# A message-passing layer on one core: TensorE's signals in the main loop carried by a drain instead of by the last matmul

## The chip, the cores and the metric

The kernel runs on one core of a Trainium2 chip. The metric is the device time of the whole program in microseconds (us), lower is better. A time is compared as the median of several runs.

The engines are called as the profile calls them: PE is TensorE (its matmuls; PEld its weight loads), DVE is VectorE, ACT is ScalarE, POOL is GpSimd, SP is SyncE, which here only issues transfers. Engines run side by side and are held together by semaphores: an instruction may wait until a semaphore has reached a value, and may raise one when it is done.

## The reference

One graph layer on 12,500 nodes of 64 features and 400,000 edges, sorted by their target node, all in f32:

```python
m_in = jnp.concatenate([x[src], x[dst], edge_attr], axis=-1)
h = jax.nn.silu(m_in @ W1 + b1)
messages = jax.nn.silu(h @ W2 + b2)
agg = jax.ops.segment_sum(messages, dst, num_segments=x.shape[0])
node_in = jnp.concatenate([x, agg], axis=-1)
u = jax.nn.silu(node_in @ W3 + b3)
y = x + u
out = (y - mean(y)) / sqrt(var(y) + 1e-5)
```

## The kernel before

The edges are taken in groups of 1024 (8 tiles of 128 edges): 390 full groups and a shorter last one, 391 in all. Everything of a group lies in a window of 48 target nodes, so the target's part of the first layer comes from a small table (`w_in`, reloaded for each group by SP) and a one-hot of 48 columns. Of a group's eight tiles of source rows `x[src]`, most are fetched by POOL with one indirect DMA per tile (seven for most groups, L547); the eighth is computed on PE: a one-hot of the source's row (`rows_T`) times the whole node table (`parts`), and DVE then picks the wanted slice out of the product (`kept`). In every twelfth group one more tile is fetched row by row by transfers that ACT issues (L674). An edge buffer `edge_in` has 12 slots, so POOL may be up to 12 groups ahead; before it refills a slot it waits for `s_in_T`, the signal of the transposes that read the slot last (`refill`, L567).

PE's step for group g is written out by hand and stands in this order:

```python
first_layer(0, g + 1)
transpose_inputs(0, g + 2)
pieces(g)
wait_for_pair(0, g)
second_layer(0, g + 1)
spread_keys(...)      # in 350 of the steps
update(...)           # a few steps per 24
sum_messages(0, g)
```

Each part ends in a signal. With the names of the rows further down (`z_ps` stands for both `z1_ps` and `z2_ps`):

- `transpose_inputs` (L1099, `in_ps`): 8 transposes; `s_in_T` lets ACT copy them out (`in_T`, L638) and POOL refill the slot.
- `first_layer` (L1120 and L1121): 2 matmuls of 512 columns into the two halves of the partitions; `s_z1` lets ACT apply the first silu (L642).
- `second_layer` (L1126): 4 matmuls; `s_z2` lets DVE add the bias (L855), ACT apply the second silu (L646), and DVE sum the messages in three passes (L866, L871, L875, L878, which makes `pair`).
- `spread_keys` (L1138): 1 matmul; `s_keys` lets DVE make the one-hot `rows_T` (L908).
- `sum_messages` (L1148): 2 small matmuls; `s_agg` lets DVE add them to `sums` (L886).
- `pick_piece` (L1165): each of the 350 computed tiles takes 26 matmuls in 13 pieces and two rounds; `s_round` at the end of a round lets DVE read it (L920, L924, which makes `kept`). A round goes to one of three PSUM banks, and its first piece waits for `s_picked`, DVE's reading of the round three before.

An f32 matmul stands in the trace as two instructions, the one-pass matmuls of `pick_piece` as one. Every engine issues in order. DVE's step for group g: bias of g + 1, `sums` of g, one-hots of g + 4, the three passes of g + 1, then `rows_T`, and the reading of the rounds.

Of the kernel before, what the change touches and what calls it, by code (L numbers as in the profile page):

```python
# [23 lines left out]
def gnn_layer(nc, x, src, dst, edge_attr, W1, b1, W2, b2, W3, b3, out):  # L24
# [3 lines left out]
    P = 128  # L28
    N, H = x.shape
# [12 lines left out]
    OH, XS, EA = slice(0, WIN), slice(WIN, WIN + H), slice(WIN + H, P)  # L42
# [11 lines left out]
    S = 12  # L54
    CH = 8
    RING = 3
    NW = 6
# [24 lines left out]
    PARTS = 2  # L82
    ROW_SETS = 3
    HB = C // H
    ROUNDS = 2
    PICK_BANKS = 3
# [43 lines left out]
    def picked(g):  # L130
        return g in PICK_OF
# [6 lines left out]
    def fetched(g):  # L138
        return g % S == 0 and 2 * S <= g < FULL
# [10 lines left out]
    def rows_landed(k, v):  # L150

        def upto(g):
            return sum(tiles_of(h) for h in range(g % S, g + 1, S))
        return 16 * upto(k * B + v)

    ctx = ExitStack()
    with ctx:
        def sb(name, shape, dt=F32):
            return ctx.enter_context(nc.sbuf_tensor(name, shape, dt))

        def pb(name, banks=()):
            return ctx.enter_context(nc.psum_tensor(name, [P, *banks, C], F32))

        def sem(name):
            return ctx.enter_context(nc.semaphore(name))
# [5 lines left out]
        parts = sb("parts", [P, PARTS, NT, H], F32R)  # L171
        edge_in = sb("edge_in", [P, S, T, P])
# [19 lines left out]
        w_in = sb("w_in", [P, NW, H])  # L192
# [30 lines left out]
        ident_r = sb("ident_r", [P, P], F32R)  # L223
        hot_place = [sb("hot_place0", [P, 2, CH, HB]), sb("hot_place1", [P, 2, CH, HB], I32)]
        kept = sb("kept", [P, HB, H])
        rows_T = sb("rows_T", [P, ROW_SETS, SETS, P], F32R)

        dst_rel = sb("dst_rel", [P, 2, CH, T])
        in_T = sb("in_T", [P, 2, C])
# [4 lines left out]
        pair = sb("pair", [P, 2, 2, H])  # L234
# [12 lines left out]
        z1_ps = pb("z1_ps")  # L247
        z2_ps = pb("z2_ps")
        agg_ps = pb("agg_ps")
        pick_ps = [pb(f"pick_ps{i}") for i in range(PICK_BANKS)]  # L250
# [34 lines left out]
        s_in_T = sem("edge_in_transposed")  # L285
        s_in_c = sem("edge_in_copied")
        s_z1 = sem("z1_done")
        s_h = sem("h_done")
        s_z2 = sem("z2_done")
# [7 lines left out]
        s_agg = sem("window_summed")  # L297
# [6 lines left out]
        s_keys = sem("keys_spread")  # L304
        s_rowsT = sem("rows_T_made")
        s_round = sem("round_done")
# [64 lines left out]
        def done(k, v):  # L371

            return k * B + (v + 1)
# [5 lines left out]
        def fetch_of(g):  # L379

            n = g // S - 2
            return n % 2, n // 2
# [681 lines left out]
        def _(pe):  # L1064
# [4 lines left out]
                             start=True, stop=True).then_inc(s_base, 1)  # L1069
# [5 lines left out]
            for n in range(len(BANKS) + 1):  # L1075
                if n < len(BANKS):
                    a, b = BANKS[n]
                    if n >= 2:
                        pe.wait_ge(s_xTc, n - 1)
                    for j in range((b - a) // 2):  # L1080
                        last = nc.tensor.transpose(in_ps[:, n % 2, j * P:(j + 1) * P],
                                                   xs[:, a + 2 * j:a + 2 * j + 2, :].rearrange("p k f -> p (k f)"), ident[:, :])
                    last.then_inc(s_xT, 1)
                if n:
                    a, b = BANKS[n - 1]
# [3 lines left out]
                    for j in range((b - a) // 2):  # L1089
                        last = nc.tensor.matmul(pick_ps[(n - 1) % 2][:, j * 2 * P:(j + 1) * 2 * P],  # L1090
                                                in_T[:, (n - 1) % 2, j * P:(j + 1) * P],
                                                w_node[:, :, :, :].rearrange("p a b f -> p (a b f)"), start=True, stop=True)
# [4 lines left out]
            def transpose_tiles(s):  # L1097
                for t in range(T):
                    last = nc.tensor.transpose(in_ps[:, t // HT, t % HT * P:(t % HT + 1) * P],  # L1099
                                               edge_in[:, s, t, :], ident[:, :])  # L1100
                return last

            def transpose_inputs(k, v):


                pe.wait_ge(s_oh, done(k, v))
                pe.wait_ge(s_eac, done(k, v))
                pe.wait_ge(s_xg[v % S], rows_landed(k, v))
                if picked(k * B + v):
                    pe.wait_ge(s_row, PICK_OF[k * B + v] + 1)  # L1110
                if fetched(v):
                    j, before = fetch_of(v)
                    for odd in range(2):
                        pe.wait_ge(s_fetched[j][odd], (before + 1) * (P // 2 * 16))
                transpose_tiles(v % S).then_inc(s_in_T, 1)

            def first_layer(k, v):
                pe.wait_ge(s_win[v % NW], k * (16 * (B // NW)) + 16 * (v // NW + 1))
                pe.wait_ge(s_in_c, done(k, v))
                nc.tensor.matmul(z1_ps[0:H, :], w_in[:, v % NW, :], in_T[:, 0, :], start=True, stop=True)  # L1120
                nc.tensor.matmul(z1_ps[H:P, :], w_in[:, v % NW, :], in_T[:, 1, :], start=True, stop=True).then_inc(s_z1, 1)  # L1121

            def by_edges():

                for c in range(HT):
                    last = nc.tensor.matmul(z2_ps[:, c * P:(c + 1) * P], h_T[:, c * P:(c + 1) * P], w2_bd[:, :],  # L1126
                                            start=True, stop=True)
                return last

            def second_layer(k, v):  # L1130
                pe.wait_ge(s_h, done(k, v))
                by_edges().then_inc(s_z2, 1)

            def spread_keys(n):

                c = TARGET[n] // CH
                pe.wait_ge(s_found, (c - TARGET[0] // CH) * 2 + 2)
                nc.tensor.matmul(agg_ps[:, KEYS], find_key[:, c % 2, TARGET[n] % CH:TARGET[n] % CH + 1].to_broadcast([P, P]),  # L1138
                                 ident_r[:, :], start=True, stop=True).then_inc(s_keys, 1)

            def wait_for_pair(k, v):

# [2 lines left out]
            def sum_messages(k, v, tail=False):  # L1145

                for i, tile in ((0, 0), (1, TT - 1 if tail else T - 1)):
                    last = nc.tensor.matmul(agg_ps[i * H:(i + 1) * H, OH], pair[:, v % 2, i, :], edge_in[:, v % S, tile, OH],  # L1148
                                            start=True, stop=True)
                last.then_inc(s_agg, 1)  # L1150

            def pick_piece(n, piece):

                r, c = PIECES[piece]
                at = n * ROUNDS + r
                a = c * PLACES + r * HB
                b = min(NT, a + HB)
                if piece == 0:
                    pe.wait_ge(s_rowsT, n + 1)
                if c == 0 and at >= PICK_BANKS:  # L1160

                    pe.wait_ge(s_picked, at - PICK_BANKS + 1)
                done_with = (r, c + 1) not in PIECES
                for j in range(PARTS):
                    last = nc.tensor.matmul(pick_ps[at % PICK_BANKS][:, 0:(b - a) * H], rows_T[:, n % ROW_SETS, c, :],  # L1165
                                            parts[:, j, a:b, :].rearrange("p k f -> p (k f)"),
                                            start=(c == 0 and j == 0), stop=(done_with and j == PARTS - 1))
                if done_with:
                    last.then_inc(s_round, 1)

            def pieces(g):
                for piece in range(PICKS * NP):
# [100 lines left out]
```

## Time and profile before

| | |
|---|---|
| time, median of 3 runs | 4534.21 us (4520.94 to 4543.54) |
| span of the profiled execution, first to last instruction | 4497.7 us |
| PE busy | 3654.5 us, 81% |
| DVE busy | 2757.0 us, 61% |
| POOL busy | 2591.6 us, 58% |
| ACT busy | 1046.2 us, 23% |

The profile gives of its execution only the span, not a device time of its own. The median of the runs is 36.5 us above the span; that is taken as what lies around it. Busy time is work that the trace records. Ends of matmuls are modelled, and where a matmul's record ends later than the next one starts, the two are pipelined.

### The profile page before, as it was taken

To read this page: it belongs to the slowest core of one execution; us is meant where nothing else is said; L and a number is where in the kernel's file an instruction comes from. 1 tells how busy PE (TensorE), PEld (TensorE's weight loads), DVE (VectorE), ACT (ScalarE), POOL (GpSimd) and SP (SyncE) were. 2 spreads that over 40 slices of the span, in tenths; PEclk is the share of its full clock that TensorE was granted. 3 is DMA by queue.
4 is the path that set the end of the run, shared out by engine and by line. 5 is a ranking of instruction groups with operands and counts; after the bars stand their busy time and mean duration, and the time that the engine had idled before them with its cause. 6 is when DMAs were issued, how large, how long until landed. Compare 5 with 4: busy or idle time off the path is not lost. (4 is left out here: it accounts for less than half of the span.)

```text
span 4497.7 us, 68074 instructions
## 1 busy us (share of the span) xinstructions
PE 3654.5 (81%) x19180; PEld 2747.4 (61%) x19180; DVE 2757.0 (61%) x4834; ACT 1046.2 (23%) x1714; POOL 2591.6 (58%) x2754
## 2 busy tenths in 40 slices
PE   1588888888888888888888888888888888888888
PEld 1366666666666666666666666666666666666665
DVE  2366666666666666666666666665665666666667
ACT  0222222222222222222222222222222222222223
POOL 7365655556555655656555555555555555555650
PEclk6789999999999999999999999999999999999998
DMA  4211111111111111111111111111111111111110
GB/s 100 59 29 34 32 28 34 33 34 29 34 33 28 34 34 30 32 28 39 28 34 28 35 32 28 33 33 33 28 33 34 28 33 28 34 32 28 38 23 11
DMA packets 335197, 150.34 MB, mean 33 GB/s; under 512 B 224958, under 2 KB 290527, under 8 KB 334822
## 3 DMA queue, kind: packets, MB, share of 16 engines
q0 software_dynamic: 87808, 90.09, 9.5%
q1 hardware_dynamic: 237238, 54.50, 5.7%
q8 instruction: 159, 2.61, 0.2%
q10 hardware_dynamic: 9776, 1.37, 0.2%
q14 instruction: 216, 1.77, 0.1%
HBM read 136.10 MB, written 9.62 MB: 32 GB/s over the span
## 5 line engine op out<-in xcount | busy, mean ns | idle before, releaser
L547 POOL DMA_INDIRECT edge_in<-in_x_dram,src_i x2744 | 2590.4, 944 | 1789.7 <-issue 743.5
L1165 PE MATMUL pick_ps<-parts,rows_T 128*128 128x512 f32 (+1 forms) x9100 | 2298.7, 405 | 564.0 <-issue 268.6
L1165 PEld LDWEIGHTS pick_ps<-parts,rows_T 128*128 128x128 f32 x9100 | 1698.8, 196 | 993.7 <-issue 384.4
L646 ACT ACTIVATE z_ps<-z_ps,zero_col 128x512 f32<-128x512 f32 x391 | 258.9, 662 | 2859.1 <-DVE z_ps L855 1975.8
L855 DVE TENSOR_TENSOR z_ps<-z_ps,b_rep 128x512 f32<-128x512 f32 x391 | 272.4, 697 | 920.9 <-remote 553.3
L1099 PEld LDWEIGHTS in_ps<-ident,edge_in 128*128 128x128 f32 x3128 | 347.7, 144 | 362.1 <-issue 341.6
L1126 PEld LDWEIGHTS z_ps<-w_bd,h_T 128*128 128x128 f32 x3128 | 471.4, 219 | 145.6 <-DVE pair L878 82.8
L1126 PE MATMUL z_ps<-w_bd,h_T 128*128 128x128 f32 x3128 | 485.7, 306 | 81.0 <-DVE pair L878 61.1
L1120 PE MATMUL z_ps<-in_T,w_in 128*64 128x512 f32 x782 | 441.2, 646 | 19.8 <-issue 14.1
L1099 PE MATMUL in_ps<-ident,edge_in 128*128 128x128 f32 x3128 | 442.4, 286 | 13.9 <-issue 7.7
L1121 PE MATMUL z_ps<-in_T,w_in 128*64 128x512 f32 x782 | 442.4, 649 | 8.6 <-issue 8.5
L638 ACT COPY in_T<-in_ps 128x1024 f32<-128x1024 f32 x391 | 394.5, 1009 | 70.9 <-remote 56.9
L908 DVE TENSOR_TENSOR rows_T<-agg_ps,key_of 128x896 fp32r<-128x896 f32 x350 | 378.6, 1082 | 0.0
L926 DVE TENSOR_REDUCE edge_in<-kept 128x64 f32<-128x512 f32 x350 | 367.8, 1051 | 12.1
L866 DVE TENSOR_REDUCE every<-z_ps 128x64 f32<-128x512 f32 x391 | 267.7, 685 | 142.0 <-ACT z_ps L646 107.6
L886 DVE TENSOR_TENSOR sums<-sums,agg_ps 128x48 f32 x391 | 79.7, 204 | 447.7 <-remote 418.2
L642 ACT ACTIVATE h_T<-z_ps,b_col 128x512 f32<-128x512 f32 x391 | 267.7, 685 | 359.3 <-remote 320.3
L871 DVE TENSOR_TENSOR z_ps<-z_ps,beyond 128x512 f32<-128x512 f32 x391 | 273.5, 699 | 13.4
L875 DVE TENSOR_REDUCE pair<-z_ps 128x64 f32<-128x512 f32 x391 | 270.2, 691 | 13.4
L924 DVE COPY_PREDICATED kept<-hot_place,pick_ps 128x512 f32<-128x512 int32 x350 | 253.6, 725 | 19.2 <-remote 4.2
L920 DVE TENSOR_TENSOR kept<-pick_ps,hot_place 128x512 f32<-128x512 f32 x350 | 239.8, 685 | 23.9 <-remote 7.3
L841 DVE TENSOR_TENSOR edge_in<-agg_ps,dst_rel 128x384 f32<-128x384 f32 x391 | 214.6, 550 | 0.4 <-issue 0.4
(104 smaller groups left out, 1231.5 us busy)
## 6 DMA issues: line engine op xcount, KB each, us to landing
edge_in<-in_x_dram ACTq DMA_DIRECT2D x3968, 0.2 KB
edge_in<-in_x_dram,src_i POOLq DMA_INDIRECT x2744
ea<-in_edge_attr_dram SPq DMA_DIRECT2D x48, 512.0 KB
w_in<-node_terms SPq DMA_DIRECT2D x391, 12.0 KB
node_terms<-h_T SPq DMA_DIRECT2D x12, 256.0 KB
node_terms<-lot_T SPq DMA_DIRECT2D x12, 256.0 KB
y<-in_x_dram SPq DMA_DIRECT2D x15, 192.0 KB
term<-node_terms SPq DMA_DIRECT2D x15, 192.0 KB
```

Source lines behind the costliest of these rows:

```text
L547: pool.indirect_dma_start(out=edge_in[:, to_slot, t, XS], out_offset=None, in_=x[:, :], in_offset=bass.IndirectOffsetOnAxis(ap=indices[:, ...
L638: nc.scalar.copy(in_T[:, :, :], in_ps[:, :, :]).then_inc(s_in_c, 1)
L855: nc.vector.tensor_add(z2, z2, b2_rep[:, :].unsqueeze(1).to_broadcast([P, T, H])).then_inc(s_biased, 1)
L871: nc.vector.tensor_mul(messages, messages, beyond[:, v // CH % 2, v % CH, :].rearrange("p (a c) -> p c a", a=2).unsqueeze(3).to_broadcast( ...
L875: nc.vector.tensor_reduce(pair[:, v % 2, 1, :], z2_ps[:, :].rearrange("p (k f) -> p f k", f=H), AX.X, ALU.add).then_inc(s_other, 1)
L908: nc.vector.tensor_tensor(rows_T[:, n % ROW_SETS, :, :], agg_ps[:, KEYS].unsqueeze(1).to_broadcast([P, SETS, P]), key_of[:, :].unsqueeze(2 ...
L926: nc.vector.tensor_reduce(edge_in[:, TARGET[n] % S, PICKED, XS], kept[:, :, :].rearrange("p k f -> p f k"), AX.X, ALU.add).then_inc(s_row, 1)
L1099: last = nc.tensor.transpose(in_ps[:, t // HT, t % HT * P:(t % HT + 1) * P], edge_in[:, s, t, :], ident[:, :])
L1120: nc.tensor.matmul(z1_ps[0:H, :], w_in[:, v % NW, :], in_T[:, 0, :], start=True, stop=True)
L1121: nc.tensor.matmul(z1_ps[H:P, :], w_in[:, v % NW, :], in_T[:, 1, :], start=True, stop=True).then_inc(s_z1, 1)
L1126: last = nc.tensor.matmul(z2_ps[:, c * P:(c + 1) * P], h_T[:, c * P:(c + 1) * P], w2_bd[:, :], start=True, stop=True)
L1165: last = nc.tensor.matmul(pick_ps[at % PICK_BANKS][:, 0:(b - a) * H], rows_T[:, n % ROW_SETS, c, :], parts[:, j, a:b, :].rearrange("p k f ...
```

## The change

Inside the main loop the semaphore increments of `transpose_inputs`, `first_layer`, `second_layer`, `spread_keys`, `sum_messages` and the ends of the rounds in `pick_piece` no longer stand on the last matmul. A drain of PE is issued behind the matmuls and carries the increment. A drain is an instruction of PE's own sequencer: it is done when the engine has finished everything before it, and what stands behind it is issued after it. The matmuls, their order, their waits and all other engines stay as they are; so do the update matmuls (`update`), and everything before the loop. Lines behind the first drain move down by one to four in the changed file.

```diff
-                transpose_tiles(v % S).then_inc(s_in_T, 1)
+                transpose_tiles(v % S)
+                pe.drain().then_inc(s_in_T, 1)
...
-                nc.tensor.matmul(z1_ps[H:P, :], w_in[:, v % NW, :], in_T[:, 1, :], start=True, stop=True).then_inc(s_z1, 1)
+                nc.tensor.matmul(z1_ps[H:P, :], w_in[:, v % NW, :], in_T[:, 1, :], start=True, stop=True)
+                pe.drain().then_inc(s_z1, 1)
...
-                by_edges().then_inc(s_z2, 1)
+                by_edges()
+                pe.drain().then_inc(s_z2, 1)
...
                 nc.tensor.matmul(agg_ps[:, KEYS], find_key[:, c % 2, TARGET[n] % CH:TARGET[n] % CH + 1].to_broadcast([P, P]),
-                                 ident_r[:, :], start=True, stop=True).then_inc(s_keys, 1)
+                                 ident_r[:, :], start=True, stop=True)
+                pe.drain().then_inc(s_keys, 1)
...
-                last.then_inc(s_agg, 1)
+                pe.drain().then_inc(s_agg, 1)
...
                 if done_with:
-                    last.then_inc(s_round, 1)
+                    pe.drain().then_inc(s_round, 1)
```

## Rows read from the trace of the kernel before

**Rows 1.** The page: the span, and each engine's busy time.

```profile
span 4497.7 us, 68074 instructions
PE 3654.5 (81%) x19180; PEld 2747.4 (61%) x19180; DVE 2757.0 (61%) x4834; ACT 1046.2 (23%) x1714; POOL 2591.6 (58%) x2754
```

**Rows 2.** Timeline, where the loop begins: start us, us, instruction [idle before <-releaser].

```profile
166.75 1.97 PE L1099 MATMUL in_ps<-ident,edge_in 128*128 128x128 f32 x8 [6.18 <-DVE edge_in L841]
```

**Rows 3.** Stretches: length, busy us (instructions) of PE, PEld, DVE, ACT, POOL; clock.

```profile
2300.00:3300.00 1000.00, 842.16 (x4413) 631.44 (x4413) 625.34 (x1091) 230.03 (x376) 589.81 (x625) 0.93 0.15 32
...
4386.50:4437.50 51.00, 50.57 (x290) 38.84 (x289) 40.02 (x66) 17.08 (x27) 0.00 (x0) 1.00 0.01 3
```

**Rows 4.** Waits of PE, 300 to 4376 us: total us, times, longest.

```profile
PE pick_ps L1165 <- DVE kept L920: 147.8, 50, 8.6
```

**Rows 5.** Timeline, one step inside the gathers.

```profile
321.56 1.05 PE L1126 MATMUL z_ps<-w_bd,h_T 128*128 128x128 f32 x8
...
322.54 0.32 PE L1148 MATMUL agg_ps<-edge_in,pair 128*64 128x48 f32 x4
...
323.66 1.09 PE L1099 MATMUL in_ps<-ident,edge_in 128*128 128x128 f32 x8
...
324.92 0.70 DVE L855 TENSOR_TENSOR z_ps<-z_ps,b_rep 128x512 f32<-128x512 f32 x1 [3.09 <-remote]
324.97 0.95 POOL L547 DMA_INDIRECT edge_in<-in_x_dram,src_i  x1 [0.30 <-issue]
...
327.83 0.69 ACT L642 ACTIVATE h_T<-z_ps,b_col 128x512 f32<-128x512 f32 x1 [1.51 <-remote]
327.87 0.20 DVE L886 TENSOR_TENSOR sums<-sums,agg_ps 128x48 f32 x1 [2.25 <-remote]
...
328.65 0.94 POOL L547 DMA_INDIRECT edge_in<-in_x_dram,src_i  x1 [2.73 <-remote]
...
332.03 1.17 PE L1165 MATMUL pick_ps<-parts,rows_T 128*128 128x512 f32 x4 [2.88 <-DVE kept L924]
```

**Rows 6.** Timeline, one step after the last gather.

```profile
4385.69 1.09 PE L1099 MATMUL in_ps<-ident,edge_in 128*128 128x128 f32 x8
...
4391.97 1.05 PE L1126 MATMUL z_ps<-w_bd,h_T 128*128 128x128 f32 x8
...
4392.78 0.30 PE L1138 MATMUL agg_ps<-ident_r,find_key 128*128 128x128 f32 x1
...
4393.01 0.32 PE L1148 MATMUL agg_ps<-edge_in,pair 128*64 128x48 f32 x4
4393.06 0.70 DVE L855 TENSOR_TENSOR z_ps<-z_ps,b_rep 128x512 f32<-128x512 f32 x1 [1.31 <-PE z_ps L1126]
...
4393.16 0.61 PE L1120 MATMUL z_ps<-in_T,w_in 128*64 128x512 f32 x1
...
4393.62 0.59 PE L1121 MATMUL z_ps<-in_T,w_in 128*64 128x512 f32 x1
...
4394.14 1.09 PE L1099 MATMUL in_ps<-ident,edge_in 128*128 128x128 f32 x8
...
4394.99 5.59 PE L1165 MATMUL pick_ps<-parts,rows_T 128*128 128x512 f32 x24
```

**Rows 7.** One line's instructions: duration ns min/median/max, first and last start.

```profile
L547 POOL DMA_INDIRECT edge_in<-in_x_dram,src_i x2744: 938/944/1323, 4.0 to 4381.2; - x196
L1165 PE MATMUL pick_ps<-parts,rows_T x9100: 218/396/797, 212.9 to 4450.3; 128*128 128x512 f32 x183, 128*128 128x128 f32 x15
```

**Rows 8.** Timeline: two places where PE restarts behind another engine's signal.

```profile
182.95 1.01 ACT L638 COPY in_T<-in_ps 128x1024 f32<-128x1024 f32 x1 [5.36 <-remote]
...
184.11 1.09 PE L1120 MATMUL z_ps<-in_T,w_in 128*64 128x512 f32 x1 [3.27 <-ACT in_T L638]
...
4484.16 0.06 DVE L1014 MEMSET done_mark<- 1x1 f32 x1
...
4484.27 3.68 PE L1181 MATMUL pick_ps<-w3a,sums 128*128 128x64 f32 x16 [0.52 <-DVE done_mark L1014]
```

More of the change, by code:

```diff
@@ L1147, in sum_messages @@
                 for i, tile in ((0, 0), (1, TT - 1 if tail else T - 1)):
-                    last = nc.tensor.matmul(agg_ps[i * H:(i + 1) * H, OH], pair[:, v % 2, i, :], edge_in[:, v % S, tile, OH],
-                                            start=True, stop=True)
-                last.then_inc(s_agg, 1)
+                    nc.tensor.matmul(agg_ps[i * H:(i + 1) * H, OH], pair[:, v % 2, i, :], edge_in[:, v % S, tile, OH],
+                                     start=True, stop=True)
+                pe.drain().then_inc(s_agg, 1)
             def pick_piece(n, piece):
@@ L1164, in pick_piece @@
                 for j in range(PARTS):
-                    last = nc.tensor.matmul(pick_ps[at % PICK_BANKS][:, 0:(b - a) * H], rows_T[:, n % ROW_SETS, c, :],
-                                            parts[:, j, a:b, :].rearrange("p k f -> p (k f)"),
-                                            start=(c == 0 and j == 0), stop=(done_with and j == PARTS - 1))
+                    nc.tensor.matmul(pick_ps[at % PICK_BANKS][:, 0:(b - a) * H], rows_T[:, n % ROW_SETS, c, :],
+                                     parts[:, j, a:b, :].rearrange("p k f -> p (k f)"),
+                                     start=(c == 0 and j == 0), stop=(done_with and j == PARTS - 1))
                 if done_with:
-                    last.then_inc(s_round, 1)
+                    pe.drain().then_inc(s_round, 1)
             def pieces(g):
```

## The prediction

> **What bounds the kernel now.** The page gives TensorE 3654.5 us of 4497.7, 81%, and no other engine over 61% [rows 1]. So PE is the busy engine, and yet it sits idle for 843 us. The loop begins at 166.8 us [rows 2] and ends where the last update matmuls begin, at 4484.3 [rows 8], so a group takes 4317.5 / 391 = 11.04 us on average.
>
> The view of stretches shows that it need not. From 4386.5 to 4437.5 us, after POOL's last gather [rows 3, 7], PE is busy 50.57 us of 51 at clock 1.00 and gets through 290 instructions, 5.7 in a us. In an ordinary stretch it is busy 842 of 1000 us at clock 0.93 and gets through 4413, or 4.4 in a us [rows 3]. The code of a step is the same in both. What differs is POOL: 590 us busy in 1000 there, 0 here.
>
> The timeline shows how POOL comes in. In the step without gathers, `second_layer` starts at 4391.97, ends by the record at 4393.02, and DVE's bias starts at 4393.06, 0.04 us later [rows 6]. In the step at 322 us `second_layer` ends at 322.61 and the bias starts at 324.92, after 3.09 us of idleness; `sum_messages` ends at 322.86 and DVE adds it at 327.87; the transposes end at 324.75 and POOL's next gather starts at 328.65, after 2.73 us of idleness [rows 5]. The last gather of that run of seven ended at 325.92, and ACT, DVE and POOL all move within 2 to 3 us of that. None of these waiters is waiting for anything but a PE signal, and PE was long past the matmul that carries it. The releaser "remote" says that no matching instruction lay near. So **while POOL issues gathers, signals carried by matmuls reach the others late by 2 to 5 us**, and in a bunch after the run.
>
> The circle closes through two waits. POOL starts the next run only on `s_in_T`, which is late until the run before is over. And DVE's reading of the rounds comes after the late bias in its own order, so PE's first piece of a round waits for `s_picked`: 2.88 us at 332.03 [rows 5], one of the waits that the list puts down to `kept` [rows 4]. Such an idle stretch also costs clock, 0.93 against 1.00 [rows 3]. A step without lateness takes 4394.14 - 4385.69 = 8.45 us with 24 pick instructions [rows 6]; the mean is 9100 / 391 = 23.3 [rows 7], each 5.59 / 24 = 0.23 us apart, so 8.29, and with the update matmuls (15 lots of 6, 180 instructions at up to 3.68 / 16 = 0.23 us [rows 8]; I take 25 us in all) 8.35 us. The lateness and what follows from it is worth 11.04 - 8.35 = 2.69 us a group, 1052 us in all.
>
> **What the change does, part by part.** It removes nothing from the matmuls. It adds per group four drains (transposes, first layer, second layer, sums), 350 / 391 for the keys and 700 / 391 for the rounds: 6.7 a group, 2614 in all.
>
> *What a drain costs on PE.* No drain stands in these rows, so it is built up. (a) The overlap is lost: the next matmul now starts before the record of the last one ends. From [rows 6]: second layer to keys 4393.02 - 4392.78 = 0.24; keys to sums 0.07 (times 0.9); sums to first layer 0.17; first layer to transposes 0.07; transposes to picks 0.24; within picks 0.396 [rows 7] less 0.23 = 0.17, times 1.8. Sum 1.09 us a group. (b) Restart: between a releasing instruction's end and PE's first matmul lie 0.05 us (4484.22 to 4484.27, the wait stands on the weight load) and 0.15 us (183.96 to 184.11, a separate wait before it) [rows 8]. A drain pays its own end and that restart, and the separate waits behind it, which PE's sequencer now works off while the matmuls in its queue still run, come into the open. Bounds: 0.1 us a drain (a restart alone) and 0.35 us (two restarts with a wait each, and 0.05). I take 0.2, since most drains have one separate wait behind them: 6.7 x 0.2 = 1.34 us. Together 2.43 us a group, 0.36 a drain; between 1.76 and 3.43.
>
> A rule speaks against the change here. The Trainium skill, "PSUM — Partial Sum Buffer", Engine vs sequencer instructions, says to put the increment on the matmul and to use a drain only for a standalone barrier, since it waits for the engine to go fully idle; the second half is what (a) and (b) charge for. It does not speak of late increments, and the trace does [rows 5].
>
> The drains lie wholly on PE's path, because PE is the engine that everyone waits for once signals are prompt; nothing hides them.
>
> *What the drains give.* The late signal is the one that a matmul carries. DVE's and ACT's own signals are taken up at once in the same stretch, and PE itself answers waits within 0.15 us, so I take it that an increment by PE's sequencer gets through during gathers. Then the 2.69 us go. What is late next: POOL has 7.02 gathers a group (2744 / 391) at 0.94 + 0.30 us [rows 5, 7], with about 0.7 us to start a run, 9.4 us, still under PE. DVE has 2757 / 391 = 7.1 us [rows 1]. So PE sets the pace, with no long idle stretch, at clock near 1.00.
>
> *The sum.* 8.35 + 2.43 = 10.78 us a group against 11.04: 391 x 0.26 = 102 us less. I give back 30 us for waits that stay (the first groups, ACT's row transfers in every twelfth). 4497.7 - 102 + 30 = 4426 of span, and with the 36.5 us around it **4460 us**, 1.6% under the median. By the bounds, 10.11 and 11.78 us a group, it is 4200 and 4850 us: two large terms of opposite sign nearly cancel.
>
> **The rivals.**
>
> *The restart is dear (slower).* Signals become prompt, but a drain and its restart cost over 0.28 us beside the overlap. The point from which it decides: 8.35 + 1.09 + 6.7 x = 11.04 gives x = 0.24 us. At 0.35 us it is 11.78 us a group, which is 290 us more than now and 30 on top: 4850. For it: in most steps one to three separate waits follow a drain. Against it: PE restarts in 0.05 to 0.15 us [rows 8].
>
> *The drain's increment is as late as the matmul's.* PE would not stand, but the circle stays and drains come on top, partly in idle time that PE has anyway (843 us less some 150 ahead of the loop, 1.8 us a group). About 12 us a group, or 375 us more: 4910. For it: I don't know which path is held. Against: PE's own matmuls run on at full rate while signals are held [rows 5], so what is held is the report, and the drain's report is another unit's.
>
> *The drain itself stands until the run of gathers is over.* Then the first drain in a run stops PE: a run of 7 x 1.25 us, 2 to 3 us behind it, and some 8 us of PE's work before the next run is released, 19 us a group: about 7700. It needs completion itself to be held, and PE's going on speaks against it.
>
> *The restart is cheap.* 0.1 us a drain or less, POOL's 9.4 us as the next bound: 4100 to 4220.
>
> **Chances.** Time differences under 0.5% (23 us) can't be told from none here. Forecast case 0.50 (of it 0.42 faster, 0.06 same, 0.02 slower; own range 4300 to 4590). Cheap restart 0.06. Dear restart 0.24 (0.02 of it same). Late drain 0.13 (0.01 same). Standing drain 0.07. That gives faster 0.48, same 0.09, slower 0.43. For the range I leave out the standing drain above and part of the cheap restart below: 4220 to 4950, which spans the bounds of the drain's cost.
>
> **What the profile after would show.** If the mechanism is right: POOL's, DVE's and ACT's waits with releaser "remote" are gone or small; the bias follows `second_layer` within 0.2 us in every stretch; PE's waits for `kept` are gone; the clock is near 1.00; between the parts of a step PE shows gaps of 0.1 to 0.5 us, at the drains; the stretch after the last gather gets slower, from 8.45 us a step to about 10.9, and equals the others. The last is the cleanest reading of a drain's price, (step - 8.45) / 7. If the stretch with gathers stays slower than the one without, signals are still held. The prediction is wrong by size if a drain costs other than 0.36 us; it is wrong by mechanism if the waiters' "remote" stays, or if PE stands for us at its drains.

## The result, and the profile after

The changed kernel takes 6359.06 us (median of 3 runs, 6339.75 to 6382.48) against 4534.21 us, a ratio of 1.404 [1.400, 1.408]: 1825 us slower, 40%. The forecast was 4460 us and the range ended at 4950.

The page of the kernel after: span and busy times, clock by fortieths of the span, and the head of the chain of work that ended last.

```profile
span 6380.6 us, 70688 instructions
PE 4669.6 (73%) x19180; PEld 3178.3 (50%) x19180; DVE 2760.7 (43%) x4834; ACT 1094.9 (17%) x1714; POOL 2594.4 (41%) x2754
...
PEclk7788788778887877887778877877888888877778
...
PEld 44%; issue 43%; PEldq 9%; DVE 2%; another core or an unknown queue 1%; DMA 0%; ACT 0%; ACTq 0%; PE 0%; DVEq 0%
```

The instructions of the engines are those of [rows 1], and 70688 - 68074 = 2614 more: the drains. PE does the same 19180 matmuls in 4669.6 us of busy time in place of 3654.5. One cause is the granted clock, 0.8 over the loop, where an ordinary stretch before had 0.93 [rows 3]; the other is that behind a drain the records no longer overlap. And 27% of the span it is idle. The chain runs almost wholly over PE (weight loads, its drains as PEldq, and "issue", time in which nothing that the profile shows is waited for).

The waits, whole span: total us, times, longest. PEq and PEldq are PE's sequencer; L1116 is the drain behind the transposes, L1135 the one behind `second_layer`, L1141 the matmul of `spread_keys`, which is the first one behind L1135.

```profile
POOL edge_in L547 <- PEq L1116: 2890.0, 373, 49.4
DVE z_ps L855 <- PEq L1135: 2777.6, 386, 19.3
...
PE agg_ps L1141 <- issue: 831.4, 349, 5.4
```

Inside the loop (300 to 6240 us) no "remote" is left: every waiter for PE now waits for a drain. But the waits are longer than before, and PE itself stands 831 us ahead of the keys' matmul, 2.4 us a time, behind the drain of `second_layer`.

One step of the timeline after, 3009 to 3030 us, with the matmuls of the picks left out:

```profile
3009.20 0.94 POOL L547 DMA_INDIRECT edge_in<-in_x_dram,src_i  x1 [0.30 <-issue]
...
3010.33 1.13 PE L1128 MATMUL z_ps<-w_bd,h_T 128*128 128x128 f32 x8 [2.06 <-issue]
...
3010.44 0.94 POOL L547 DMA_INDIRECT edge_in<-in_x_dram,src_i  x1 [0.30 <-issue]
...
3013.02 0.70 DVE L855 TENSOR_TENSOR z_ps<-z_ps,b_rep 128x512 f32<-128x512 f32 x1 [5.90 <-PEq L1135]
...
3013.19 0.45 PE L1141 MATMUL agg_ps<-ident_r,find_key 128*128 128x128 f32 x1 [1.74 <-issue]
...
3014.41 1.09 PE L1121 MATMUL z_ps<-in_T,w_in 128*64 128x512 f32 x1 [0.24 <-issue]
...
3016.72 1.94 PE L1099 MATMUL in_ps<-ident,edge_in 128*128 128x128 f32 x8 [0.34 <-issue]
...
3019.45 0.94 POOL L547 DMA_INDIRECT edge_in<-in_x_dram,src_i  x1 [8.07 <-PEq L1116]
...
3026.78 1.05 PE L1128 MATMUL z_ps<-w_bd,h_T 128*128 128x128 f32 x8
3026.95 0.94 POOL L547 DMA_INDIRECT edge_in<-in_x_dram,src_i  x1 [0.30 <-issue]
...
3029.40 0.70 DVE L855 TENSOR_TENSOR z_ps<-z_ps,b_rep 128x512 f32<-128x512 f32 x1 [10.47 <-PEq L1135]
```

This is the circle. `second_layer` is through by the record at 3011.46, but its drain ends only at 3013.0, when the bias starts: 1.6 us after the last gather (3011.38). Only then do keys, sums, `first_layer` and transposes follow, each with its drain, 5.7 us to the end of the transposes (3018.66), with matmuls at half clock (1.09 us for what takes 0.61 in [rows 6]; 1.2 of 2.4 GHz). POOL, idle for 8.07 us, starts its next run at 3019.45; it lasts until 3027.89; the next `second_layer`, at 3026.78, falls into its end, and its drain stands until 3029.4. From release to release 16.4 us.

Two stretches, as in [rows 3]: us, then busy us (instructions) of PE, PEld, DVE, ACT and POOL, clock, DMA share, GB/s. The second lies after the last gather.

```profile
2300.00:3300.00 1000.00, 755.11 (x3026) 514.03 (x3027) 435.18 (x761) 170.51 (x264) 408.09 (x433) 0.79 0.12 22
...
6260.00:6310.00 50.00, 44.02 (x222) 31.01 (x221) 31.29 (x51) 14.61 (x23) 0.00 (x0) 1.00 0.01 2
```

And two transposes in that second stretch:

```profile
6259.80 1.06 PE L1099 MATMUL in_ps<-ident,edge_in 128*128 128x128 f32 x8 [0.23 <-issue]
...
6270.77 1.06 PE L1099 MATMUL in_ps<-ident,edge_in 128*128 128x128 f32 x8 [0.34 <-issue]
```

Without gathers a step takes 10.97 us at clock 1.00. With them it is 15.85 us: L1135's drains start first at 174.7 and last at 6357.2 us, 390 steps apart. The 10.97 was forecast ("about 10.9"); the 15.85 was not.

A finer count of the same trace. From the end of the last matmul's record to the end of the drain behind it is 0.02 us where nothing is held; what is more than that is taken as standing. Summed, that is 859 us for `second_layer` (2.20 us each), 144 for the rounds, 44 for the sums and 26 for the other three kinds: 1073 us. By which gather of a run of six or seven POOL was in when the work was done, the share of drains that stood over 0.3 us was 0 to 1% in the first three, 21% in the fourth, and 66, 85 and 80% in the fifth to seventh. For signals on matmuls in the kernel before, where the reader already sat idle when the work was done, it was 0 of 8 in the second gather, 4 of 11 in the third, 85% in the fourth and 64 to 97% behind it. Of what was held over 1 us in the changed kernel, 69% ended 1.5 to 2.5 us after the run. So in the loop completion on PE is reported late from the third or fourth gather in a row, mostly until some 2 us after the run, whoever carries the report.

That is not a switch which the fourth gather throws. Longer runs hold for longer: in the changed kernel the held drains end, in the median, 1.56, 1.76 and 1.98 us behind runs of six, seven and eight. In the setup of the kernel before POOL issues 93 gathers in a row, from 4.0 to 120.3 us. There DVE still takes up a matmul's result promptly in the 24th (L813 at 34.22 us, and at 34.27 in c_before, where nothing is held). Two gathers on, the next is 7 us late (43.53 against 36.41). Then ACT waits up to 16.1 us a time, and reports are let through one by one while the gathers go on. They are late behind the run as well. PE's last work here ends at 118.55 us, and ACT's next copy, which waits for PE alone, starts at 131.74, at least 13 us late and 11 us after the last gather:

```profile
117.92 0.63 PE L1081 MATMUL in_ps<-ident,sums 128*128 128x128 f32 x2
...
119.31 0.95 POOL L547 DMA_INDIRECT edge_in<-in_x_dram,src_i  x1 [0.30 <-issue]
...
131.74 0.37 ACT L615 COPY in_T<-in_ps 128x256 f32<-128x256 f32 x1 [15.44 <-remote]
```

That looks more like a backlog that a run builds up and a pause works off; nothing here tests it.

### The profile page after: what moved, and what is told of

It reads as the page before. It is cut to its first block, busy times and chain, and to the rows that moved or that the text cites. A ratio compares the mean times of both kernels' runs of the same rounds, so it can differ in the third digit from the quotient of the medians.

```text
span 6380.6 us, 70688 instructions
## 1 busy us (share of the span) xinstructions
PE 4669.6 (73%) x19180; PEld 3178.3 (50%) x19180; DVE 2760.7 (43%) x4834; ACT 1094.9 (17%) x1714; POOL 2594.4 (41%) x2754
## 4 chain that ended last, share of the span: by engine, by line
PEld 44%; issue 43%; PEldq 9%; DVE 2%; another core or an unknown queue 1%; DMA 0%; ACT 0%; ACTq 0%; PE 0%; DVEq 0%
PEld pick_ps L1169 26%; PEld in_ps L1099 8%; PEld z_ps L1128 6%; PEldq L1173 2%; PEldq L1135 2%; PEldq L1123 1%; PEld agg_ps L1141 1%; PEldq L1143 1%; PEld agg_ps L1152 1%; PEld z_ps L1121 1%; PEldq L1154 1%; PEldq L1116 1%; PEld z_ps L1122 0%; PEld agg_ps L1185 0%
## 5 line engine op out<-in xcount | busy, mean ns | idle before, releaser
L1169 PE MATMUL pick_ps<-parts,rows_T 128*128 128x512 f32 (+1 forms) x9100 | 2578.4, 433 | 242.4 <-issue 187.7
L1169 PEld LDWEIGHTS pick_ps<-parts,rows_T 128*128 128x128 f32 x9100 | 1849.0, 213 | 945.6 <-issue 538.3
L855 DVE TENSOR_TENSOR z_ps<-z_ps,b_rep 128x512 f32<-128x512 f32 x391 | 273.5, 700 | 2802.0 <-PEq L1135 2777.6
L1099 PEld LDWEIGHTS in_ps<-ident,edge_in 128*128 128x128 f32 x3128 | 549.4, 204 | 700.1 <-issue 570.6
L1099 PE MATMUL in_ps<-ident,edge_in 128*128 128x128 f32 x3128 | 675.4, 388 | 146.1 <-issue 138.1
L1121 PE MATMUL z_ps<-in_T,w_in 128*64 128x512 f32 x782 | 650.9, 929 | 137.4 <-issue 136.2
L1141 PE MATMUL agg_ps<-ident_r,find_key 128*128 128x128 f32 x350 | 130.0, 371 | 831.5 <-issue 831.4
L1122 PE MATMUL z_ps<-in_T,w_in 128*64 128x512 f32 x782 | 663.8, 946 | 0.0
L1141 PEld LDWEIGHTS agg_ps<-ident_r,find_key 128*128 128x128 f32 x350 | 82.0, 234 | 891.6 <-issue 891.6
L1128 PE MATMUL z_ps<-w_bd,h_T 128*128 128x128 f32 x3128 | 439.6, 286 | 69.0 <-issue 62.8
L1128 PEld LDWEIGHTS z_ps<-w_bd,h_T 128*128 128x128 f32 x3128 | 424.5, 200 | 118.5 <-issue 80.5
```

Of the source, the lines that this page charges most:

```text
L855: nc.vector.tensor_add(z2, z2, b2_rep[:, :].unsqueeze(1).to_broadcast([P, T, H])).then_inc(s_biased, 1)
```

## The experiments

Where a kernel has fewer gathers, or narrower ones, the rows `x[src]` that they would bring are missing from the edge inputs, and its output is another; everything else is computed on what lies in the slot. Kernels of one set ran on one chip beside the kernel before, whose time in that set is given.

### The drain's price without gathers: a_none, b_none

```diff
-        return TT if g == FULL else T - picked(g) - fetched(g)
+        whole = TT if g == FULL else T - picked(g) - fetched(g)
+        return whole if g < S else min(whole, 0)
```

The first 12 groups are still gathered, those after not at all: in the changed kernel (a_none) and in the one before (b_none).

> The changed kernel with all its drains, but from group 12 on POOL gathers no rows (those tiles keep what an earlier group left in the slot, so the output is another one). Theory (during a run of gathers the completion of matmuls is not reported, and a drain makes PE stand for it): every drain becomes cheap, 0.36 us beside the matmul's own slot, and the step is 10.8 to 11.0 us, in all 4400 to 4550 us, with PE's clock near 1.0. Rival (a drain and its restart are dear on their own): the step stays near 15.9 us, in all over 6000 us.

> The kernel before, signals on the matmuls, with the same gathers left out. Theory (gathers hold back the signals, and nothing else slows the loop): 8.4 us a step as in the stretch after the last gather, in all 3450 to 3600 us. Rival (the late signals come from somewhere else, such as the rows that ACT fetches or the load of the instruction queues): 4300 us or more. The difference to the same kernel with drains is 2614 times the price of a drain without gathers; theory: 900 to 1050 us.

Measured: 4428.97 us (0.983 [0.981, 0.985] of before, 4506.61) and 3521.65 us (0.781 [0.780, 0.783]). The difference is 907.3 us over 2614 drains: **0.347 us a drain**, 2.32 us a group. So with gathers the kernel before takes 985 us more than without, and the changed one 1930 us more (6359.06 is of another set of runs).

The drain of `second_layer` in a_none: duration min/median/max in ns from its place in the queue, first and last start.

```profile
L1136 PEldq DRAIN  x391: 973/2382/3390, 176.5 to 4403.6; - x196
```

(4403.6 - 176.5) / 390 = 10.84 us a step: the step after the last gather, now everywhere.

### How many gathers in a run: a_three, a_five

The edit is the one above on the changed kernel with `min(whole, 3)` and `min(whole, 5)`.

> The changed kernel, but from group 12 on POOL gathers three tiles a group in place of seven (the others are left out). In both traces signals and drains are prompt in the first three gathers of a run and late from the fourth on, until about 1.8 us after its end. Theory (the hold needs a run of more than three gathers): hardly a drain stands, 11.0 to 11.6 us a step, 4450 to 4700 us. Rival (any gather holds completion, and the time held goes with their number): about 3/7 of the way from no gathers to seven, so 5100 to 5400 us.

> The changed kernel with five gathers a group from group 12 on (the others are left out). Theory (the hold begins at the fourth gather in a row and lasts until about 1.8 us after the last): the drains behind the fourth gather stand, but 2.5 us a step less long than with seven, 12.5 to 13.5 us a step, 5050 to 5450 us. Rival (the hold needs the whole run of seven): near 4450 us.

Measured: 4433.41 us (0.984 [0.982, 0.985]) with three a group, 4 us from none at all, though POOL is busy 1162 us there. With five 4983.17 us (two runs, 1.098 [1.095, 1.101], before 4534.93 in that set), 554 us over a_none. So three gathers a group cost nothing, the next two 554 us and the last two 1376, as the count by gather said. Both times lie a little below the range expected. The wait for the drain of `second_layer`, here L1136, in a_five:

```profile
DVE z_ps L856 <- PEq L1136: 1765.2, 390, 10.3
```

1765 us, against 2777.6 with seven and 1277 in a_none.

### What it is about the gathers: a_busy, a_thin

a_busy is a_none with 14 memsets of the unused `msg` per group, so that POOL is busy without a gather:

```diff
-                    fill(k, v, tiles)
+                    for _ in range(14):
+                        nc.gpsimd.memset(msg[:, :, :, :], 0.0).then_inc(s_spin, 1)
+                        spun[0] += 1
+                        pool.wait_ge(s_spin, spun[0])
```

a_thin is the changed kernel with gathers of 16 of the 64 features, a quarter of the bytes in as many rows:

```diff
-                        out=edge_in[:, to_slot, t, XS], out_offset=None, in_=x[:, :],
+                        out=edge_in[:, to_slot, t, WIN:WIN + thin[0]], out_offset=None, in_=x.rearrange("n (a f) -> (n a) f", f=thin[0]),
```

> The changed kernel with no gathers from group 12 on, but POOL writes a scratch tile 14 times a group in their place (no transfer). Theory (the gathers' transfers or descriptors hold completion, POOL's being busy doesn't): as with no gathers, 4400 to 4550 us. Rival (POOL being busy without a pause is enough): over 5000 us.

> The changed kernel; from group 12 on each gather fetches 16 of the 64 features of a row (of other rows, so the output is another one): as many gathers and rows, a quarter of the bytes. Theory A (the number of gathers or of their rows holds completion): 6200 to 6450 us as with all bytes. Theory B (the bytes written to SBUF do): under 5200 us.

Measured, two runs each: a_busy 4428.56 us (0.976 [0.973, 0.979]), the same as a_none within 0.5 us, with POOL busier than in any kernel here:

```profile
PE 3787.1 (86%) x19180; PEld 2658.9 (60%) x19180; DVE 2797.3 (63%) x4834; ACT 1093.1 (25%) x1714; POOL 2875.1 (65%) x5395
```

a_thin 6261.72 us (1.390 [1.385, 1.395], before 4505.22): nearly all of it stays. So it isn't POOL's being busy, and hardly the bytes moved. It goes with the indirect gathers; whether with their issue, their 128 rows each or the reports of their landing is not told apart.

### Which drain it is: a_z2mm, b_tdrain, b_z2drain, d_z2drain

a_z2mm is the changed kernel with the signal of `second_layer` back on its matmul. b_tdrain and b_z2drain are the kernel before with a single kind of drain, that of the transposes or that of `second_layer`:

```diff
-                transpose_tiles(v % S).then_inc(s_in_T, 1)
+                transpose_tiles(v % S)
+                pe.drain().then_inc(s_in_T, 1)
...
-                by_edges().then_inc(s_z2, 1)
+                by_edges()
+                pe.drain().then_inc(s_z2, 1)
```

> The changed kernel with one signal undone: the second layer's is back on its last matmul, all other drains stay. Of the time that drains stand beyond their matmuls, 853 of about 1244 us is at the second layer's. Theory (completion as such is held, so the next drain, a fraction of a us behind, stands in its place): only the drain's own 0.4 us a step goes, 6150 to 6300 us. Rival (the second layer's drain is dear because of what stands there): over 2 us a step go, 5300 to 5600 us.

> The kernel before with one part of the change: only the signal of the transposes is carried by a drain. Theory (release comes 1.8 us after POOL's run, whoever carries the signal): PE stands at this drain until the release, POOL's run of 8.8 us begins 0.7 us behind it, so the step is 8.8 + 0.7 + 1.8 = 11.3 us or a little over, 4600 to 4850 us. Rival (the stand of some 2.4 us comes on top of the step): 13 us a step or more, over 5200 us.

> The kernel before with one part of the change: only the second layer's signal is carried by a drain. Theory (PE stands at this drain until the release and has not issued the transposes yet, so POOL's next run waits for PE's part behind the drain, and PE and POOL work in turn): release to transposes done 1.9 us at the full clock and 3.9 us at the half one, start of POOL 0.7, run 8.8, release 1.8: 13.2 to 15.2 us a step, 5300 to 6000 us. Rival (a drain costs what it stands, 2.2 us a step, partly in PE's idle 1.8 us): 11.4 to 13 us a step, 4600 to 5250 us.

Measured: a_z2mm 6019.75 us (1.335 [1.333, 1.338], before 4506.61). Only 339 us come back, more than the 60 to 210 that were expected and far less than the rival's 760, for the next drain inherits the standing: PE now waits ahead of the sums, which are the first thing behind the keys' drain.

```profile
POOL edge_in L547 <- PEq L1116: 2553.1, 373, 49.2
...
PE agg_ps L1151 <- issue: 810.0, 302, 5.2
```

This run also shows both carriers side by side. `second_layer` ends at 3010.89 with its signal on the matmul, the keys behind it at 3010.95 with a drain, and bias and sums start within 0.07 us of each other, 3.6 us later:

```profile
3014.52 0.70 DVE L855 TENSOR_TENSOR z_ps<-z_ps,b_rep 128x512 f32<-128x512 f32 x1 [8.02 <-remote]
...
3014.59 0.45 PE L1151 MATMUL agg_ps<-edge_in,pair 128*64 128x48 f32 x4 [3.64 <-issue]
```

Of the 279 drains of the keys that stood over 1 us, 241 ended within 0.15 us of the bias's start. **What is held is the completion, and it holds signal and drain alike.**

b_tdrain 4532.60 us (1.006 [1.004, 1.009], before 4505.22). That is below the 4600 to 4850 expected. The drain of the transposes does stand, 533 us in sum by the count above or 1.36 us each, and yet costs 27 us in all. Its signal comes no later than the matmul's did: POOL waits 1076.8 us for it, and for the matmul it was 649.2 and 395.1 us (under "remote" and under the line itself). Behind it stand only the picks, in front of which PE was idle anyway ([rows 4, 5]); that this slack is what takes the standing up is argued, not shown.

b_z2drain gave 3579.59 us, and the kernel before in that set 3466.96 us, in place of the 4505 to 4535 of all sets until then: 1.033 [1.031, 1.034]. Both expectations spoke of a chip on which signals are held, and here none was. The next section is on that. The same kernel was run once more, and that set had the kernel before at 4507.14 us:

> The kernel before with the drain of the second layer alone, in one more set. Where the kernel before takes about 3467 us: 3575 to 3585 us, as twice so far. Where it takes about 4500 us, so that completion is held while POOL gathers: my theory says that this drain, which stands ahead of sums, first layer and transposes in PE's order, stands until about 1.8 us after a run of gathers and so puts the whole step behind it, 5300 to 6000 us. Rival: a single standing drain is hidden where reports are held, since the bias is late there with and without it, 4520 to 4700 us.

Measured: 5493.04 us, 1.218 [1.214, 1.222]. Its timeline, again without the picks:

```profile
3011.43 1.05 PE L1126 MATMUL z_ps<-w_bd,h_T 128*128 128x128 f32 x8
...
3014.54 0.94 POOL L547 DMA_INDIRECT edge_in<-in_x_dram,src_i  x1 [0.30 <-issue]
...
3017.24 0.47 PE L1139 MATMUL agg_ps<-ident_r,find_key 128*128 128x128 f32 x1 [4.76 <-issue]
...
3019.76 1.97 PE L1099 MATMUL in_ps<-ident,edge_in 128*128 128x128 f32 x8
...
3022.50 0.95 POOL L547 DMA_INDIRECT edge_in<-in_x_dram,src_i  x1 [7.01 <-PE in_ps L1099]
```

The drain holds PE for 4.76 us, until 1.7 us after the run's last gather (3015.48). The transposes, behind it, release POOL 5.3 us later. **One drain makes the circle**: +986 us, where the drain of the transposes, which hasn't them behind it, costs 27. Between these two kinds the place in PE's order decides.

### Letting the reports through: a_split, b_split, b_split5

POOL stops behind the third (a_split, b_split) or fifth gather (b_split5) of a fill until these have landed:

```diff
+                if pause:
+                    gather(src_i[:, q, column_of, :], v % S, pause, s_xg[v % S])
+                    pool.wait_ge(s_xg[v % S], rows_landed(k, v) - 16 * (tiles - pause))
+                    pool.nop(nofuse=True)
+                gather(src_i[:, q, column_of, :], v % S, tiles, s_xg[v % S], pause)
```

> The changed kernel with all its gathers, but POOL stops behind the third of a run until those three have landed, and then issues the other four. Theory (what counts is the number of gathers in a row without a pause, and it starts anew): hardly a drain stands, and the step is 11 to 12.5 us, set by the drains' own price or by POOL's 8.8 us of gathers and two starts, 4500 to 5100 us. Rival (the number or the bytes of gathers per step counts, pause or not): 6000 us or more.

> The kernel before, signals on the matmuls, with the same stop of POOL behind the third gather. Theory: signals are prompt most of the time, PE has 8.4 us of work a step, and POOL sets the pace with 8.8 us of gathers, a start of 0.7 us and a stop of 1.2 to 2 us: 10.7 to 11.6 us a step, 4380 to 4700 us, and the waits without a releaser are small. Rival (signals are late whatever the pause): 11.0 us and the stop on top, 5000 us or more.

> The kernel before with POOL's stop behind the fifth gather of a group in place of the third. Theory (POOL, no longer waiting for the transposes' late signal, issues seven gathers between two stops wherever the stop lies, 8.8 us and a stop of 2 us): 10.7 us a step, 4330 to 4400 us, as with the stop behind the third. Rival (the place of the stop against PE's step matters): another time by over 1%.

Measured: a_split 5168.82 us (1.141 [1.137, 1.145], before 4534.93), 1190 us better than the changed kernel, but over the 4500 to 5100 expected. By the count above drains still stand 531 us, for the runs join across groups: 222 have four gathers and 93 have seven. b_split 4345.41 us, 0.957 [0.954, 0.960], and b_split5 4295.42 us, **0.954 [0.951, 0.957]** (before 4505.22), each some 35 us under its range: the best of all where reports are held. The ratios don't tell the place of the stop apart. The stop in b_split5, timeline:

```profile
3005.17 0.95 POOL L547 DMA_INDIRECT edge_in<-in_x_dram,src_i  x1 [0.30 <-issue]
...
3008.39 0.95 POOL L547 DMA_INDIRECT edge_in<-in_x_dram,src_i  x1 [2.26 <-issue]
```

After its stop of 2.26 us POOL goes straight on into the next fill, so the gathers join across groups into seven in a row again, and signals are still held (DVE waits 455.1 us for the bias under "remote", 553.3 in the kernel before). What has changed is POOL's pause: one of 2.26 us that waits for its own gathers, in place of one of 2.73 us that waits for late transposes [rows 5]. POOL sets the pace in both: 7.02 gathers at 1.25 us are 8.8 us, and the steps, from the matmuls of `second_layer` (first at 173.6, last at 4478.6 us before, 175.0 and 4274.1 in b_split5), are 11.04 and 10.51 us.

### The same kernels where nothing is held: c_before, c_after, c_z2drain, c_split5

After b_z2drain's surprise the kernel before, the changed one and two of the above were run word for word in one set.

> The kernel before, unchanged, with a profile of its own in this set. If it takes about 4500 us, its profile repeats the late reports (DVE idle ahead of the bias, PE idle ahead of the rounds, clock 0.93). If it takes about 3467 us, the bias starts within 0.1 us of the second layer's end also while POOL gathers, the clock is near 1.00, and PE is busy over 95%. The rival to a held report would be that the 1000 us come from slower gathers: POOL's gathers would then be longer or further apart than 0.945 and 0.30 us at 4500 us, and they are not longer in the 3578 us profile of the kernel with one drain.

> The changed kernel once more, word for word, because the kernel before has shown two times: 4495 to 4553 us in three sets of runs, and 3467 us in one. My theory: the kernel before at 3467 us is one in which completion of matmuls is reported at once in spite of the gathers, and 4500 us one in which it is held. Where the kernel before takes about 4500 us, the drains stand with the held reports and this takes 6250 to 6420 us. Where it takes about 3467 us, nothing is held and only the drains' own price is paid, 2614 at 0.35 us: 4350 to 4430 us. Rival: the late reports come from the matmuls' number or the kernel's own pattern, then the changed kernel takes 6250 to 6420 us whatever the kernel before shows.

> The kernel before with the drain of the second layer alone, once more. Theory: where the kernel before takes about 4500 us, this one drain stands until the run of gathers is over, sums and transposes come behind it, and POOL's next run is released by them: 5300 to 6000 us. Where it takes about 3467 us: 3575 to 3585 us again. Rival: a single standing drain is hidden also where reports are held, as that of the transposes was: 4520 to 4700 us beside 4500.

> The kernel before, POOL stopping behind the fifth gather of each fill until it has landed, once more. Theory: the stop is a gain only because it lets held reports through. Beside 4500 us: 4280 to 4310 again. Beside 3467 us, where nothing is held, it costs: POOL's seven gathers at 1.25 us and a stop of 2.2 us make 10.9 us a group against 8.8, 4100 to 4350 us. Rival: the stop relieves the DMA queues and gains in either case.

Measured, the kernel before at 3467.20 us (3465.77 to 3468.57, 7 runs): c_before 3466.80 us (one run); c_after 4340.40 us, 1.252 [1.250, 1.254]; c_z2drain 3579.97 us, 1.033 [1.031, 1.034]; c_split5 4249.78 us, 1.226 [1.224, 1.228]. c_after is 10 us under its range, the others are in theirs.

c_before, its span and busy times, a stretch, and a step of its timeline inside gathers:

```profile
span 3465.0 us, 68074 instructions
PE 3333.6 (96%) x19180; PEld 2571.0 (74%) x19180; DVE 2790.0 (81%) x4834; ACT 1057.1 (31%) x1714; POOL 2597.9 (75%) x2754
```

```profile
1000.00:2000.00 1000.00, 989.33 (x5717) 765.57 (x5716) 823.89 (x1420) 307.71 (x496) 756.02 (x801) 1.00 0.22 41
```

```profile
2502.69 0.95 POOL L547 DMA_INDIRECT edge_in<-in_x_dram,src_i  x1 [0.30 <-issue]
...
2503.25 1.05 PE L1126 MATMUL z_ps<-w_bd,h_T 128*128 128x128 f32 x8
2503.94 0.94 POOL L547 DMA_INDIRECT edge_in<-in_x_dram,src_i  x1 [0.30 <-issue]
...
2504.34 0.70 DVE L855 TENSOR_TENSOR z_ps<-z_ps,b_rep 128x512 f32<-128x512 f32 x1 [1.17 <-PE z_ps L1126]
```

POOL's gathers are the same, 0.95 us and 0.30 between them, and run without a pause. But the bias starts 0.04 us after `second_layer`, as in [rows 6] it did only without gathers; PE is busy 989 us of 1000 at clock 1.00 and does 5.7 instructions in a us, the rate of the undisturbed stretch in [rows 3]. Nor are the transfers slower where reports are held: a gather's packets take 93 ns on average in c_before and 78 in the kernel before. So the 1067 us between 3467 and 4534 go with the held reports; nothing else was found to differ.

c_after, its waits and the drain of `second_layer`:

```profile
DVE z_ps L855 <- PEq L1135: 1270.6, 390, 7.9
POOL edge_in L547 <- PEq L1116: 851.4, 345, 4.6
```

```profile
L1135 PEldq DRAIN  x391: 972/2388/3390, 87.9 to 4313.1; - x196
```

Here (4313.1 - 87.9) / 390 = 10.83 us a step, as in a_none without gathers. None of the 2614 drains stands by the count above (no time differs by 0.02 us from the fastest of its kind). Its `second_layer` drains begin at 87.9 us in place of 176.5, so the setup, too, had been paying for held reports while POOL filled the 12 slots; that is the 89 us by which a_none was longer. And the change costs (4340.4 - 3467.2) / 2614 = **0.334 us a drain**, with nothing to give back.

c_split5's waits show why the stop turns into a loss: POOL waits 896 us for its rows to land, and PE then 615 us for gathered rows.

```profile
POOL edge_in L547 <- DMA edge_in<-in_x_dram,src_i: 895.7, 377, 4.4
...
PE in_ps L1103 <- DMA edge_in<-in_x_dram,src_i: 614.7, 298, 6.5
```

Its step is (4224.2 - 87.4) / 390 = 10.61 us, within 1% of b_split5's 10.51 with held reports. With POOL's own pause in it the loop hardly depends on the reports any more.

## Why the prediction was wrong

**Right: what bounds the kernel.** That signals come late while POOL gathers, that the lateness closes a circle over POOL's run and DVE's readings, and that a step without it takes about 8.35 us. b_none takes 3521.65 us, and c_before shows the same kernel, gathers and all, at 8.61 us a step: (3446.1 - 87.5) / 390 from the matmuls of `second_layer`. That is 0.26 us more than forecast. In c_before PE is the bound, as was said of prompt signals.

**Right: what a drain costs on PE.** 2.43 us a group, 0.36 a drain, between 1.76 and 3.43. Measured 2.32 (a_none less b_none) and 2.23 (c_after less c_before), 0.35 and 0.33 a drain; a drain of `second_layer` alone 0.29 us (112.8 / 391 in c_z2drain). The two parts came out too: from c_before to c_after PE's busy time grows by 444.2 us, 1.14 us a group of lost overlap against 1.09, and its idle time by 426.8 us, 1.09 against 1.34 for the restarts. The stretch after the last gather reads 10.97 us a step against "about 10.9". The Trainium skill, "PSUM — Partial Sum Buffer", Engine vs sequencer instructions, has the increment put on the matmul and keeps the drain for a standalone barrier. It gives correctness as the reason and no price. The price here is in c_after: 873 us more with nothing but drains added and nothing held.

**Wrong: what the drains give.** "I take it that an increment by PE's sequencer gets through during gathers. Then the 2.69 us go." They didn't; 5.01 us a group came on top (15.85 - 10.84). The reason given was that the sequencer answers waits at once and PE's matmuls run on. Both are true of [rows 5], and neither tells what a drain waits for. A drain needs the report of completion itself, and that is what is held, as a_z2mm shows. As long as the signal sat on a matmul, only its reader waited and PE ran on: in [rows 5] the transposes are already done at 324.75 when the held signals come. With a drain PE waits too, and the transposes are not even begun. Of the 5.01 us, 1073 / 391 = 2.74 are drains that stand, by the count above. The rest is clock: PE's busy time is 4669.6 us, against 3777.8 in c_after for the same matmuls and drains, 2.28 us a group. The sum, 5.02, closes. In the prediction's own terms: 8.35 + 2.43 became 8.35 + 2.49 without gathers (10.84), and the term for lateness, -2.69 against the 11.04 of before, became +5.01 on top of that.

**The rival that was nearest had 0.07.** "The drain itself stands until the run of gathers is over" named the mechanism, its place and the circle, and put it at 19 us a group. It is 15.85: the parts were a run of 8.75 us, 2 to 3 us behind it and 8 us of PE's work, and in the step shown they are 8.4, 1.5 and 6.4 us (3019.45 to 3027.89, to 3029.4, and 3013.0 to 3019.45). It was set aside on "PE's going on speaks against it", the same misreading. The rival "late drain" assumed that PE wouldn't stand (1.8 us of idle time to hide in); the wait at L1141 refutes it.

**Wrong in what would tell.** "POOL's, DVE's and ACT's waits with releaser 'remote' are gone" was meant as proof of prompt signals. They are gone from the loop, and the signals are later: the label went with matmuls as releasers. Only the lengths tell.

**One small term had no ground.** The 36.5 us "around the span" are not around it. In the runs that list both, the time is 1.9 us above the span (6382.48 and 6380.6 for the changed kernel), so the profiled execution of the kernel before took about 4499.6 us, less than all three of the runs behind the median. Without that the sum would have read about 4428; no verdict hangs on it.

**The cause under it is open.** The sum rested on a lateness of 2.69 us that isn't the kernel's. Of the seven sets with the kernel before beside them, five had it at 4505 to 4535 us and two at 3467, with like gathers, and d_z2drain's set, at 4507, came after those two, so it isn't a drift. Nor is it the chip by the number under which the record lists it: number 1 had the kernel before at 4534.93 us in a_five's set and at 3466.96 in b_z2drain's, though the number may name another chip on another machine. What differs no row shows. Nor do the rows show which path is blocked. That in the loop it mostly ends some 2 us after the last gather's record, about when gathered rows land (2.26 us in b_split5), fits a report that shares something with the gathers' transfers; the 11 us in the setup do not fit that alone. By the Trainium skill, "Perfetto Trace Analysis", DMA Instruction — SWDGE (GPSIMD), a gather's record ends with the making of its descriptors and not with the data, and the 2.26 us from that end to POOL's restart on the landing agree. But a_thin's quarter of the bytes changed little, and why three in a row are free in the loop, and some 25 in the setup, was not found.

## What to carry to other kernels

If a signal comes late although its work is done, find out whether the signal or the completion behind it is late before changing its carrier: one drain in the loop, at the place with the most behind it, answers that. A drain turns a late report into a stop of the engine, so what matters is what stands behind it in that engine's order, above all whatever releases the engine that causes the lateness. And measure the kernel before in every set: one and the same kernel took 3467 us and 4534 us here, and the stop that gained 4.6% in the one case lost 22.6% in the other.

## What the runs showed of the hardware

- While POOL issues indirect gathers of 0.945 us with 0.30 between them, completion on PE is reported late in five of seven sets. In the loop runs of three cost nothing (a_three 4433 us against 4429 without any); drains stand from the fourth on (21% there, 66 to 85% behind it), 4.76 us in d_z2drain's step. In a setup with 93 gathers in a row the first 24 cost nothing, and a report let through 11 us behind the last one was at least 13 us late. Signals on matmuls and drains are held alike (a_z2mm: 241 of 279 let go together). A busy POOL without gathers (65%, a_busy) does nothing of the kind.
- The same program took 3467 us in two sets and 4505 to 4535 us in five (medians), with gathers of 946 and 944 ns on average.
- A drain with its restart costs PE 0.33 to 0.35 us on average in this loop at full clock, 0.29 us where it stands behind `second_layer` alone.
- Standing costs twice: with PE idle 27% of the span the granted clock falls from 1.00 (c_after) to 0.79, and matmuls behind a long stop run at the lower of the two levels, 1.09 us for 0.61.
